# A fused FFN, GRU and expert kernel on one core: the loop over tiles and the loop over weight pieces written out

## The chip, the cores and the metric

The kernel runs on one core of a Trainium2 chip. The metric is the device time of one execution in microseconds (us). Five engines of the core work side by side and meet at semaphores only: TensorE (PE, with its weight loads as PEld), VectorE (DVE), ScalarE (ACT), GpSimd (POOL) and SyncE (SP, which here only issues DMAs).

## What is computed

The reference joins two blocks over x of 16 sequences, 256 steps, 512 features. Cut to what matters:

```python
# block 0: attention over 8 block sums gives one row per sequence; layer norm; FFN on quantised values
proj = attended @ Wo.T
q = layernorm(x + proj) * ln_gamma + ln_beta
inter = silu(q8(q) @ q4(w_gate).T) * (q8(q) @ q4(w_up).T)      # 512 -> 2048
x = x + q8(inter) @ q4(w_down).T                               # 2048 -> 512
# block 1: a GRU over the 256 steps, h is [16, 512]; then a linear layer with routed low-rank experts
for t in range(256):
    gi, gh = x[:, t] @ W_ih + b_ih, h @ W_hh + b_hh
    r, z = sigmoid(gi_r + gh_r), sigmoid(gi_z + gh_z)
    n = tanh(gi_n + r * gh_n)
    h = (1 - z) * n + z * h
    hs[:, t] = h
logits = silu(hs @ rw1.T + rb1) @ rw2.T + rb2 + gates
coeff = softmax of the two largest logits, the rest 0          # 16 experts, rank 16
x = x + hs @ W.T + bias + expand(hs @ A.T, coeff) @ B
```

The 256 steps of the GRU depend on each other one by one; all else can run beside them.

## The kernel before, in words

A tile is 8 time steps times 16 sequences, 128 rows, and there are 32 tiles. The work is a software pipeline over a counter c: while the GRU takes the 8 steps (slots s = 0 to 7) of tile c, the same slots carry quantisation of tile c+4 (flag Q), the FFN of tile c+3 and the end of the FFN of tile c+2 (F, E), the input products `gi` of tile c+1 (I), and the routed experts and output of tile c-1 (L). Flag R says that the GRU itself runs. For c from 1 to 27 all six flags are set.

Each engine has its own program, written in order by one `slot(c, s)` per engine; the order is fixed by hand. In a slot of PE `state_products` comes first: 64 matmuls into `ps_rn` and 32 into `ps_z` (L1299), which need the state parts `hx` of the step before. Behind it stand the other products of the slot. DVE does `beside(0)` (FFN work), then `recur` (r_half L739, r_pre L745, z_pre L755, rn L760, n_pre L762, zn L772, hx L774, and last the low part `hx` L725, which releases the next step on PE and POOL), with `beside(1)` and `beside(2)` inside it, and `beside(3)` at its end. ACT does the tanh of r, z and n, and evictions. POOL copies `hx` into `hT_steps` (L1016), collects a tile in `hT_tile` (L1023, once a tile), multiplies scales into quantised tiles (`qf` L1003, `qx` L1051), and does small steps of the routing (`share` L1035, `c` L1040, `coeff` L1044). SP loads and stores the tiles.

`over_tiles` calls `slot` for c = -3 to 1 as written-out code, then puts one loop on every engine (`engine.Fori(2, TILES - 5)`, so c = 2 to 26, 25 turns, its line in the trace is L275) whose counter is a register, and then c = 27 to 32 written out again. Before that, `over_pieces` quantises and turns the FFN weights in 24 pieces; pieces 8 to 11 stand in a loop of two turns (L293), the others are written out. In a loop every wait is for a value worked out from the counter: `count(c, per_tile, more)`. Where a wait of such a value stands before some instructions, `wait_apart` adds one increment of a semaphore `passed`, which nobody waits for, between the wait and the instruction. These increments are in the written-out tiles too. On DVE they stand before `to_f8` (L799), before `clip` (L806), before `bn_aggr`, `max` and `max_index`; on POOL before both copies of h, before `ve`, `share` and each `c`; on PE before `turn_hid`; on SP before each load and store.

Of the kernel before, what the change touches and what calls it, by code (L numbers as in the profile page):

```python
# [63 lines left out]
def count(tile, per_tile, more=0):  # L64

    if isinstance(tile, int):
        if tile < 0:
            return 0
        if tile >= TILES:
            return TILES * per_tile  # L70
    return tile * per_tile + more


def wait(engine, sem, value):

    if not (isinstance(value, int) and value <= 0):
        engine.wait_ge(sem, value)


def wait_apart(engine, passed):  # L80


    engine.sem_inc(passed, 1)
# [11 lines left out]
def build(nc, x_steps, h0, ident, pick, block_mask, iota, rms_w, query, WkT, WoT, gamma, beta,  # L95
          ffn_w, W_ih, W_hh, b_ih, b_hh, WL, bias, rb1, rw2T, rb2, gates, BT, x1_dram, out):
    with ExitStack() as ctx:
# [164 lines left out]
        passed = sem("passed")  # L262
# [23 lines left out]
        def over_pieces(engine, piece, sums, attention, slot, ahead=0):  # L286
# [35 lines left out]
        def stages(c):  # L322


            if not isinstance(c, int):
                return True, True, True, True, True, True
            return tuple(0 <= c + d < TILES for d in (4, 3, 2, 1, 0, -1))
# [3 lines left out]
        def _(sp):  # L331

            def piece(turn, u):
                wait(sp, w_y, count_piece(turn, u, -1))
                wait_apart(sp, passed)
                at = (turn * 2 + u) * P
                src = ffn_w[at:at + P, :] if isinstance(turn, int) else ffn_w[bass.ds(at, P), :]
                sp.dma_start(wst[u][:, :], src).then_inc(w_loaded[u], 16)

            def loads(c):  # L340
                Q, F, E, I, R, L = stages(c)
                if L:
                    wait(sp, x1b_done, count(c - 1, 1))
                    wait_apart(sp, passed)
                    sp.wait_ge(x1_stored, count(c, 1) * 16)
                    wait_apart(sp, passed)
                    sp.dma_start(x1_in[:, :], rows(x1_dram, c - 1)).then_inc(x1in_loaded, 16)
                if E:
                    wait(sp, x1_done, count(c + 2, 1))
                    wait_apart(sp, passed)  # L350
                    sp.dma_start(xres[:, :], rows(x_steps, c + 2)).then_inc(xres_loaded, 16)

            def load_x_in(q):
                wait(sp, xs_done, count(q, 1))
                wait_apart(sp, passed)
                sp.dma_start(xin[:, :], rows(x_steps, q)).then_inc(xin_loaded, 16)

            def stores(c):
                Q, F, E, I, R, L = stages(c)
                if E:  # L360
                    sp.wait_ge(x1_done, count(c + 2, 1, 1))
                    wait_apart(sp, passed)
                    sp.dma_start(rows(x1_dram, c + 2), x1[:, :]).then_inc(x1_stored, 16)
                if L:
                    sp.wait_ge(y_ok, count(c - 1, 1, 1))
                    wait_apart(sp, passed)
                    sp.dma_start(rows(out, c - 1), y[:, :]).then_inc(y_stored, 16)

            def rows(dram, t):
                if isinstance(t, int):  # L370
                    return dram[t * P:(t + 1) * P, :]
                return dram[bass.ds(t * P, P), :]

            def slot(c, s):
                if s == 0:
                    loads(c)
                    if isinstance(c, int) and c == -4:
                        load_x_in(0)
                if s == 4 and (not isinstance(c, int) or c + 5 < TILES):
                    load_x_in(c + 5)  # L380
                if isinstance(c, int) and c == -4:
# [5 lines left out]
                if isinstance(c, int) and c == -3 and s == STEPS - 2:  # L387
# [8 lines left out]
            over_pieces(sp, piece, nothing, nothing, slot)  # L396
            over_tiles(sp, slot)
# [5 lines left out]
        def _(act):  # L403
# [27 lines left out]
            def piece(turn, u):  # L431
                ps = (ps_up, ps_z)[u]
                act.wait_ge(w_mm, count_piece(turn, u, 1))
                nc.scalar.activation(wq[:, bass.ds(turn * 2 + u, 1), :], ps[:, :].bitcast(BF16).unsqueeze(1),
# [46 lines left out]
            def others(c, s, Q, F, E, I, L):  # L481
# [45 lines left out]
                if I and s in (1, 3, 5):  # L527
                    g = s // 2
                    act.wait_ge(gi_mm, count(i, 3, g + 1))
                    if isinstance(c, int) and c == -1:  # L530
# [6 lines left out]
            def slot(c, s):  # L537
# [9 lines left out]
                if isinstance(c, int) and c in (-3, -2, 0):  # L547
# [3 lines left out]
            over_pieces(act, piece, load_x, attention, slot, ahead=1)  # L551
            over_tiles(act, slot)
# [3 lines left out]
        def _(dve):  # L556
# [16 lines left out]
            def piece(turn, u):  # L573


                if not (isinstance(turn, int) and turn == TURNS - 1 and u == 1):
# [225 lines left out]
            def clip(out, in8, ready, at, used, done):  # L802
                wait(dve, used, at)
                dve.wait_ge(ready, at + 1)
                wait_apart(dve, passed)
# [26 lines left out]
            def others(c, s, place, Q, F, E, I, L):  # L832
# [15 lines left out]
                if L and here == (4, 2):  # L848
                    dve.wait_ge(l_small, count(l, 6, 2))
                    wait_apart(dve, passed)  # L850
                    v.max(top[:, :], lg[:, :]).then_inc(l_small, 1)
                if L and here == (5, 1):
                    dve.wait_ge(l_small, count(l, 6, 3))
                    wait_apart(dve, passed)
# [42 lines left out]
                if Q and here == (1, 0):  # L897
# [5 lines left out]
                    wait_apart(dve, passed)  # L903
# [26 lines left out]
            def slot(c, s):  # L930
# [11 lines left out]
                if isinstance(c, int):  # L942
                    if c == -3:
                        gru_weights(s)
                    if c in (-2, 0):
                        input_weights(c, s)
# [5 lines left out]
            over_pieces(dve, piece, nothing, attention, slot)  # L952
            over_tiles(dve, slot)
# [3 lines left out]
        def _(pool):  # L957
# [22 lines left out]
            def piece(turn, u):  # L980

                if not (isinstance(turn, int) and turn == TURNS - 1 and u == 1):
# [5 lines left out]
            def slot(c, s):  # L988
                Q, F, E, I, R, L = stages(c)
                q, f, e, l = c + 4, c + 3, c + 2, c - 1  # L990
                if Q and s == 0:
                    pool.wait_ge(xin_loaded, count(q, 16, 16))
                    wait(pool, xn_done, count(q, 1))
                    if isinstance(c, int) and c == -4:
# [16 lines left out]
                if R:  # L1011
# [3 lines left out]
                    wait_apart(pool, passed)  # L1015
                    g.tensor_copy(hT_steps[:, :, s, :], hx[:, :, :, :].rearrange("p k u b -> p (k u) b"))\  # L1016
                        .then_inc(hcopy, 1)
                if R and s == STEPS - 1:
# [3 lines left out]
                    wait_apart(pool, passed)  # L1022
# [8 lines left out]
                if L and s == 5:  # L1031
                    pool.wait_ge(gap_ok, count(l, 1, 1))
                    wait_apart(pool, passed)
# [3 lines left out]
                    for place, c_one in enumerate((c0, c1)):  # L1037
                        pool.wait_ge(share_ok, count(l, 2, 2))
                        wait_apart(pool, passed)
# [15 lines left out]
            over_pieces(pool, piece, nothing, attention, slot)  # L1055
            over_tiles(pool, slot)
# [3 lines left out]
        def _(pe):  # L1060
# [156 lines left out]
            def turn_hid(l):  # L1217
                pe.wait_ge(hid_ok, count(l, 1, 1))
                pe.wait_ge(xa_ok, count(l, 1, 1))
                wait_apart(pe, passed)  # L1220
# [101 lines left out]
            def slot(c, s):  # L1322
# [6 lines left out]
                if isinstance(c, int):  # L1329
                    if c in (-3, -2):  # L1330
                        weights_scales(c, s)
                    if (c, s) == (-1, 0):
# [66 lines left out]
```

## Time and profile before

| | |
|---|---|
| time, median of 3 runs | 1940.21 us (1937.06 to 1950.23) |
| time of the profiled execution | 1945.7 us |
| span of the profiled execution, first to last instruction | 1943.9 us |
| PE busy | 1646.0 us, 85% |
| DVE busy | 1597.8 us, 82% |
| ACT and POOL busy | 664.4 us and 654.8 us, 34% each |

The profile divides the span into 40 slices of 48.6 us and gives busy tenths of each engine for a slice. The first six or so are the weights and the attention; from there the tiles run, one in about a slice. A busy PE is not a PE at its peak, since ends of its matmuls are modelled.

### The profile page before, as it was taken

Reading aid. Unit: us, or ns where it says so; the run is one execution under the profiler, and the core shown is the slowest. Engines: PE = TensorE matmul, PEld = TensorE weight load, DVE = VectorE, ACT = ScalarE, POOL = GpSimd, SP = SyncE. Lnnn points to the kernel's source line nnn. Section 1 sums busy time; section 2 is a strip of 40 time slices with the busy share of each in tenths; the row PEclk is TensorE's granted clock in tenths of the full one; section 3 lists DMA queues with packets and bytes.
Section 4 is the critical chain, followed back from the end, with each engine's and each line's share of the span. In section 5 each row is a group of like instructions: output and inputs, shape, how many; then the busy total and the mean of one; then the engine's idle time right before and its main releaser. Section 6 shows DMA issues by size and latency. Waiting matters only on the chain. (4 is left out here: it accounts for less than half of the span.)

```text
span 1943.9 us, 81883 instructions
## 1 busy us (share of the span) xinstructions
PE 1646.0 (85%) x32972; PEld 1247.0 (64%) x32972; DVE 1597.8 (82%) x5651; ACT 664.4 (34%) x1712; POOL 654.8 (34%) x859
## 2 busy tenths in 40 slices
PE   5422348999999999999999999999999999999976
PEld 2211116777777777777777777777777777778864
DVE  8999987888888888888788888888888888887653
ACT  1111224433333333333333333333333333333331
POOL 4555323333333333333323333333333333332111
PEclk8755569999999999999999999999999999999997
DMA  7413120000000000001000000000000000001000
GB/s 254 147 60 125 51 87 24 25 30 31 30 30 30 30 30 27 12 30 30 30 30 30 30 30 25 30 30 30 30 30 30 30 30 17 22 26 32 27 14 18
DMA packets 35405, 80.45 MB, mean 41 GB/s; under 512 B 4864, under 2 KB 5248, under 8 KB 34688
## 3 DMA queue, kind: packets, MB, share of 16 engines
q1 hardware_dynamic: 28080, 63.09, 9.6%
q10 hardware_dynamic: 6992, 12.13, 1.7%
q8 instruction: 306, 5.01, 1.1%
q14 instruction: 27, 0.22, 0.0%
HBM read 58.43 MB, written 16.78 MB: 39 GB/s over the span
## 5 line engine op out<-in xcount | busy, mean ns | idle before, releaser
L1299 PE MATMUL ps_rn<-hx,whh 128*128 128x32 f16 x16384 | 451.1, 176 | 77.1 <-DVE hx L725 47.5
L1299 PEld LDWEIGHTS ps_rn<-hx,whh 128*128 128x128 f16 x16384 | 430.8, 96 | 124.9 <-DVE hx L725 93.7
L1016 POOL COPY hT_steps<-hx 128x128 f16<-128x128 f16 x256 | 120.0, 469 | 978.7 <-DVE hx L725 978.7
L1192 PE MATMUL ps_gi<-x1T,wih 128*128 128x128 f16 x4608 | 288.6, 219 | 1.2 <-ACT gi L533 1.2
L1192 PEld LDWEIGHTS ps_gi<-x1T,wih 128*128 128x128 f16 x4608 | 270.3, 98 | 25.7 <-issue 1.7
L542 ACT ACTIVATE r_tanh<-r_pre,scale_half 128x64 f32<-128x64 f32 x256 | 89.0, 348 | 563.3 <-DVE r_pre L745 563.3
L1299 PE MATMUL ps_z<-hx,whh 128*128 128x32 f16 x8192 | 244.0, 176 | 0.0
L1299 PEld LDWEIGHTS ps_z<-hx,whh 128*128 128x128 f16 x8192 | 223.4, 96 | 0.0
L533 ACT ACTIVATE gi<-ps_gi,b_i,scale_x 128x128 f32 (+1 forms) x384 | 144.7, 457 | 166.2 <-PE ps_gi L1192 166.2
L1003 POOL TENSOR_TENSOR qf<-f8c,fe 128x512 bf16<-128x512 bf16 x128 | 135.8, 1061 | 119.3 <-DVE f8c L806 102.7
L1125 PE MATMUL ps_gate_up<-wq,qxT 128*128 128x512 bf16 x512 | 144.2, 398 | 32.3 <-issue 19.8
L739 DVE TENSOR_TENSOR r_half<-ps_rn,gi 128x64 f32<-128x64 f32 x256 | 55.9, 218 | 111.5 <-PE ps_rn L1299 111.0
L1131 PE MATMUL ps_gate_up<-wq,qxT 128*128 128x512 bf16 x512 | 136.3, 390 | 1.7 <-ACT sg_gs L493 1.7
L1149 PE MATMUL ps_down<-wq,qfT 128*128 128x512 bf16 x512 | 134.8, 386 | 0.0
L544 ACT ACTIVATE z_tanh<-z_pre,scale_half 128x64 f32<-128x64 f32 x256 | 89.0, 348 | 123.7 <-DVE z_pre L755 123.7
L806 DVE TENSOR_SCALAR f8c<-f 128x512 bf16<-128x512 fp8e4 x128 | 109.8, 858 | 17.8 <-DVE f L799 0.2
L546 ACT ACTIVATE n<-n_pre,scale_half 128x64 f32<-128x64 f32 x256 | 89.1, 348 | 57.5 <-DVE n_pre L762 44.0
L762 DVE SCALAR_TENSOR_TENSOR n_pre<-gi,rn 128x64 f32<-128x64 f32 x256 | 75.7, 296 | 30.6 <-DVE rn L760 0.2
L1201 PE MATMUL ps_base<-wl,hT_tile 128*128 128x512 f16 x384 | 98.0, 393 | 0.0
L799 DVE SCALAR_TENSOR_TENSOR f<-inter,finv 128x512 fp8e4<-128x512 f32 x128 | 94.0, 734 | 0.3
L821 DVE TENSOR_TENSOR inter<-ps_gate_up,sg_gs 128x512 f32<-128x512 f32 x128 | 87.8, 686 | 7.2 <-PE ps_gate_up L1131 7.1
L493 ACT ACTIVATE sg_gs<-ps_gate_up 128x512 f32<-128x512 f32 x128 | 74.7, 583 | 53.4 <-PE ps_gate_up L1125 53.3
(197 smaller groups left out, 2765.5 us busy)
## 6 DMA issues: line engine op xcount, KB each, us to landing
wih<-in_x_steps ACTq DMA_DIRECT2D x32, 256.0 KB, 5.4
xin<-in_x_steps SPq DMA_DIRECT2D x32, 256.0 KB, 4.1
xres<-in_x_steps SPq DMA_DIRECT2D x32, 256.0 KB, 4.1
x_dram<-x SPq DMA_DIRECT2D x32, 256.0 KB, 2.8
x_in<-x_dram SPq DMA_DIRECT2D x32, 256.0 KB, 2.8
out_rows<-y SPq DMA_DIRECT2D x32, 256.0 KB, 2.0
wst<-in_ffn_w SPq DMA_DIRECT2D x12, 512.0 KB, 3.2
sg_gs<-in_ffn_w SPq DMA_DIRECT2D x12, 512.0 KB, 3.5
```

The lines of the kernel that those rows point to most:

```text
L533: last = nc.scalar.activation(gi_gate(i, g)[:, k, :], ps_gi[:, k * P:(k + 1) * P], ACT.Identity, bias=b_i[:, g * KD + k:g * KD + k + 1], s ...
L546: nc.scalar.activation(n[:, :], n_pre[:, :], ACT.Tanh, scale=HALF_S_INV).then_inc(n_ok, 1)
L799: v.scalar_tensor_tensor(blocked(out8[:, :]), blocked(src[:, :]), TO_F8, spread(inverse[:, :]), ALU.mult, ALU.mult, saturate=False).then_i ...
L806: v.tensor_scalar(out[:, :], in8[:, :], 7.5 / 64, -7.5 / 64, ALU.min, ALU.max).then_inc(done, 1)
L1003: g.tensor_tensor(blocked(qf[:, :]), blocked(f8c[:, :]), spread(fe16[:, :]), ALU.mult).then_inc(qf_done, 1)
L1016: g.tensor_copy(hT_steps[:, :, s, :], hx[:, :, :, :].rearrange("p k u b -> p (k u) b"))\
L1125: last = mm(ps_gate[:, :], qxT[:, k, :], w_ffn(0, n, k), start=k == 0, stop=k == KD - 1)
L1131: last = mm(ps_up[:, :], qxT[:, k, :], w_ffn(8, n, k), start=k == 0, stop=k == KD - 1)
L1149: last = mm(ps_down[:, :], qfT[:, i, :], w_down(i), start=i == 0, stop=i == NF * KD - 1)
L1192: last = mm(ps_gi[:, j * P:(j + 1) * P], wih_parts[:, k, at:at + P], x1T[:, x, k, :], start=k + w + x == 0, stop=k == KD - 1 and w == 1)
L1201: last = mm(out, hT_tile[:, 2 * k + x, :], wl_parts[:, k, begin:begin + n], start=k + w + x == 0, stop=stop and w == 1)
L1299: last = mm(ps[:, (at + j) * 2 * B:(at + j + 1) * 2 * B], whh[:, k, u, gate * D + j * P:gate * D + (j + 1) * P], hx[:, k, :, :].rearrange( ...
```

## The change

The loops on the engines become Python loops, so all 25 turns of the tile loop and both turns of the piece loop are written out as code. No counter register is left: every wait is for a constant. `wait_apart` and the semaphore `passed` are gone, everywhere. No instruction that computes is added, removed or moved. The core of the diff; the same lines go at the other places named above:

```diff
 def wait(engine, sem, value):
 
-    if not (isinstance(value, int) and value <= 0):
+    if value > 0:
         engine.wait_ge(sem, value)
-
-
-def wait_apart(engine, passed):
-
-
-    engine.sem_inc(passed, 1)
...
-        def over_tiles(engine, slot):
-
-            def all_slots(c):
+        def over_tiles(slot):
+
+            for c in range(-3, TILES + 1):
                 for s in range(STEPS):
                     slot(c, s)
 
-            for c in range(-3, 2):
-                all_slots(c)
-            with engine.Fori(2, TILES - 5) as c:
-                all_slots(c)
-            for c in range(TILES - 5, TILES + 1):
-                all_slots(c)
...
-            with engine.Fori(SUM_PARTS // 2, TURNS // 2) as turn:
-                piece(turn, 0)
-                piece(turn, 1)
+            for p in range(SUM_PARTS, PIECES // 2):
+                piece(p // 2, p % 2)
...
-            if isinstance(c, int):
-                at = (c % 2 * 3 + gate) * D
-                part = gi[:, at:at + D]
-            else:
-                part = gi[:, bass.ds((c & 1) * (3 * D) + gate * D, D)]
+            at = (c % 2 * 3 + gate) * D
+            part = gi[:, at:at + D]
...
                 if E:
                     wait(sp, x1_done, count(c + 2, 1))
-                    wait_apart(sp, passed)
                     sp.dma_start(xres[:, :], rows(x_steps, c + 2)).then_inc(xres_loaded, 16)
...
             def clip(out, in8, ready, at, used, done):
                 wait(dve, used, at)
                 dve.wait_ge(ready, at + 1)
-                wait_apart(dve, passed)
                 v.tensor_scalar(out[:, :], in8[:, :], 7.5 / 64, -7.5 / 64, ALU.min, ALU.max).then_inc(done, 1)
...
                     for place, c_one in enumerate((c0, c1)):
                         pool.wait_ge(share_ok, count(l, 2, 2))
-                        wait_apart(pool, passed)
                         g.tensor_scalar(c_one[:, :], iota_b[:, :], at_f[:, place:place + 1], share[:, place:place + 1],
```

PE, end of a turn and start of the next slot: `x_row` gives the spread scale, `bt` the experts, `x` and `qx` are turned, and `ps_rn` opens the next step. Before, at the end of the loop's body (what follows the branch here is the code behind the loop; a taken branch goes back to such a `ps_rn` row at the top):

```order
L1129 REGISTER_ALU
L1131 MATMUL ps_gate_up<-wq,qxT 128x512 x4
L1169 MATMUL ps_turn<-idf,x 128x128 x4
L1149 MATMUL ps_down<-wq,qfT 128x512 x4
L1173 REGISTER_ALU
L1180 MATMUL ps_route<-idb,qx 128x128 x4
L275 REGISTER_ALU
L275 COMPARE_AND_BRANCH
L1299 MATMUL ps_rn<-hx,whh 128x32 x64
```

The same place in the changed kernel, which now stands there once for each tile:

```order
L1089 MATMUL ps_gate_up<-wq,qxT 128x512 x4
L1127 MATMUL ps_turn<-idf,x 128x128 x4
L1107 MATMUL ps_down<-wq,qfT 128x512 x4
L1138 MATMUL ps_route<-idb,qx 128x128 x4
L1256 MATMUL ps_rn<-hx,whh 128x32 x64
```

The matmuls are the same in the same order; register work and branch are gone. PE's body has 27 rows of register work, a loop's frame included.

DVE, the recurrence of one step inside the loop before:

```order
L739 ISA
L739 TENSOR_TENSOR r_half<-ps_rn,gi 128x64
L741 TENSOR_TENSOR hn_half<-ps_rn,b_h 128x64
L745 TENSOR_TENSOR r_pre<-ps_rn,r_half 128x64
L748 TENSOR_TENSOR hn<-ps_rn,hn_half 128x64
L752 ISA
L752 TENSOR_TENSOR z_half<-ps_z,gi 128x64
L755 TENSOR_TENSOR z_pre<-ps_z,z_half 128x64
L760 SCALAR_TENSOR_TENSOR rn<-r_tanh,hn 128x64
L762 ISA
L762 SCALAR_TENSOR_TENSOR n_pre<-gi,rn 128x64
```

And the same rows of the changed kernel:

```order
L708 TENSOR_TENSOR r_half<-ps_rn,gi 128x64
L710 TENSOR_TENSOR hn_half<-ps_rn,b_h 128x64
L714 TENSOR_TENSOR r_pre<-ps_rn,r_half 128x64
L717 TENSOR_TENSOR hn<-ps_rn,hn_half 128x64
L721 TENSOR_TENSOR z_half<-ps_z,gi 128x64
L724 TENSOR_TENSOR z_pre<-ps_z,z_half 128x64
L729 SCALAR_TENSOR_TENSOR rn<-r_tanh,hn 128x64
L731 SCALAR_TENSOR_TENSOR n_pre<-gi,rn 128x64
```

An ISA row here is register work on the counter. In the body of DVE's loop 70 of 239 rows are register work or the branch; the other 169 stand in the changed kernel once for each tile. Increments of `passed` have no rows in this listing.

## Rows read from the trace of the kernel before

**Rows 1.** The page: busy tenths of PE in 40 slices, and TensorE's granted clock.
```profile
PE   5422348999999999999999999999999999999976
...
PEclk8755569999999999999999999999999999999997
```
**Rows 2.** Who waited for whom: engine, line, releaser, us in total, times, longest.
```profile
PEld ps_rn L1299 <- DVE hx L725: 93.7, 131, 2.5
```
**Rows 3.** DVE in order of time, L725 only: start, us, engine, line, operation.
```profile
369.27 0.22 DVE L725 TENSOR_TENSOR hx<-h,hx 128x64 f16<-128x64 f32 x1
...
398.18 0.22 DVE L725 TENSOR_TENSOR hx<-h,hx 128x64 f16<-128x64 f32 x1
...
403.55 0.23 DVE L725 TENSOR_TENSOR hx<-h,hx 128x64 f16<-128x64 f32 x1
...
415.59 0.22 DVE L725 TENSOR_TENSOR hx<-h,hx 128x64 f16<-128x64 f32 x1
...
464.78 0.22 DVE L725 TENSOR_TENSOR hx<-h,hx 128x64 f16<-128x64 f32 x1
...
1699.24 0.23 DVE L725 TENSOR_TENSOR hx<-h,hx 128x64 f16<-128x64 f32 x1
...
1729.71 0.22 DVE L725 TENSOR_TENSOR hx<-h,hx 128x64 f16<-128x64 f32 x1
...
1735.43 0.22 DVE L725 TENSOR_TENSOR hx<-h,hx 128x64 f16<-128x64 f32 x1
...
1747.46 0.22 DVE L725 TENSOR_TENSOR hx<-h,hx 128x64 f16<-128x64 f32 x1
```
**Rows 4.** Stretch of tile 27: us, busy us of PE, PEld, DVE, ACT, POOL, clock, DMA.
```profile
1699.50:1747.70 48.20, 47.13 (x1021) 37.35 (x1020) 41.85 (x169) 19.20 (x52) 16.98 (x25) 1.00 0.08 25
```
**Rows 5.** The loops' lines: durations ns min/median/max, first and last start us.
```profile
L275 PEldq COMPARE_BRANCH  x25: 76/3430/3915, 464.3 to 1698.8; - x25
...
L275 DVEq COMPARE_BRANCH  x25: 50/56/74, 466.7 to 1701.2; - x25
...
L293 PEldq COMPARE_BRANCH  x2: 76/162/247, 91.4 to 108.2; - x2
```
**Rows 6.** PE in order of time behind the loop's branch, a turn's end.
```profile
1085.42 0.39 PE L1180 MATMUL ps_route<-idb,qx 128*128 128x128 bf16 x4
1086.72 1.76 PE L1299 MATMUL ps_rn<-hx,whh 128*128 128x32 f16 x64 [0.91 <-issue]
```
**Rows 7.** PE in order of time at the same place in written-out code.
```profile
1749.52 0.39 PE L1180 MATMUL ps_route<-idb,qx 128*128 128x128 bf16 x4
1749.74 1.75 PE L1299 MATMUL ps_rn<-hx,whh 128*128 128x32 f16 x64
```
**Rows 8.** DVE in order of time, tile 27, with its waits.
```profile
1718.06 0.68 DVE L799 SCALAR_TENSOR_TENSOR f<-inter,finv 128x512 fp8e4<-128x512 f32 x1
1718.88 1.53 DVE L806 TENSOR_SCALAR f8c<-f 128x512 bf16<-128x512 fp8e4 x1
...
1724.35 0.68 DVE L821 TENSOR_TENSOR inter<-ps_gate_up,sg_gs 128x512 f32<-128x512 f32 x1
1725.07 0.69 DVE L780 TENSOR_REDUCE fam<-inter 128x16 f32<-128x512 f32 x1
...
1733.17 0.09 DVE L855 MATCH_VALUE_LOAD top_at<-top,lg 128x8 f32 x1 [0.26 <-issue]
...
1737.89 1.47 DVE L863 TENSOR_TENSOR wxa<-xa,coeff 128x256 f32<-128x256 f32 x1 [0.56 <-POOL coeff L1044]
```
**Rows 9.** The page, DMA queues that bring instructions: packets, MB, share.
```profile
q8 instruction: 306, 5.01, 1.1%
q14 instruction: 27, 0.22, 0.0%
```
**Rows 10.** POOL in order of time, tile 27.
```profile
1718.86 1.27 POOL L1028 TENSOR_TENSOR xg<-xn,gamma_b 128x512 f32<-128x512 f32 x1
...
1721.50 1.05 POOL L1003 TENSOR_TENSOR qf<-f8c,fe 128x512 bf16<-128x512 bf16 x1
...
1736.69 0.86 POOL L1040 TENSOR_SCALAR c<-iota_b,at_f,share 128x16 f32<-128x16 f32 x2 [0.21 <-POOL share L1035]
```
**Rows 11.** Line L806: durations ns min/median/max, first and last start.
```profile
L806 DVE TENSOR_SCALAR f8c<-f x128: 426/428/1542, 232.0 to 1802.6; 128x512 bf16<-128x512 fp8e4 x128
```

More of the change, by code:

```diff
@@ L284, in count_piece, with over_pieces @@
             return turn * 2 + (u + more)
-        def over_pieces(engine, piece, sums, attention, slot, ahead=0):
+        def over_pieces(piece, sums, attention, slot, ahead=0):
             for p in range(SUM_PARTS):
@@ L376, in slot @@
                     loads(c)
-                    if isinstance(c, int) and c == -4:
+                    if c == -4:
                         load_x_in(0)
-                if s == 4 and (not isinstance(c, int) or c + 5 < TILES):
+                if s == 4 and c + 5 < TILES:
                     load_x_in(c + 5)
-                if isinstance(c, int) and c == -4:
+                if c == -4:
                     if s == 3:
@@ L394, in slot @@
                     stores(c)
-            over_pieces(sp, piece, nothing, nothing, slot)
-            over_tiles(sp, slot)
+            over_pieces(piece, nothing, nothing, slot)
+            over_tiles(slot)
             sp.wait_ge(y_stored, 16 * TILES)
@@ L546, in slot @@
                     nc.scalar.activation(n[:, :], n_pre[:, :], ACT.Tanh, scale=HALF_S_INV).then_inc(n_ok, 1)
-                if isinstance(c, int) and c in (-3, -2, 0):
+                if c in (-3, -2, 0):
                     weights(c, s)
                 others(c, s, Q, F, E, I, L)
-            over_pieces(act, piece, load_x, attention, slot, ahead=1)
-            over_tiles(act, slot)
+            over_pieces(piece, load_x, attention, slot, ahead=1)
+            over_tiles(slot)
         @block.vector
@@ L573, in piece @@
             def piece(turn, u):
-                if not (isinstance(turn, int) and turn == TURNS - 1 and u == 1):
+                if not (turn == TURNS - 1 and u == 1):
                     scales(turn + u, 1 - u)
@@ L951, in _ @@
             scales(0, 0)
-            over_pieces(dve, piece, nothing, attention, slot)
-            over_tiles(dve, slot)
+            over_pieces(piece, nothing, attention, slot)
+            over_tiles(slot)
         @block.gpsimd
@@ L980, in piece @@
             def piece(turn, u):
-                if not (isinstance(turn, int) and turn == TURNS - 1 and u == 1):
+                if not (turn == TURNS - 1 and u == 1):
                     scale_piece(turn + u, 1 - u)
@@ L1054, in _ @@
             scale_piece(0, 0)
-            over_pieces(pool, piece, nothing, attention, slot)
-            over_tiles(pool, slot)
+            over_pieces(piece, nothing, attention, slot)
+            over_tiles(slot)
         @block.tensor
@@ L1328, in slot @@
                     state_products(ps_z, 0, GATE_Z).then_inc(z_mm, 1)
[L1329 to L1332, printed above, removed]
-                        pe.wait_ge(wih_lo, KD)
-                    if (c, s) == (1, 0):
-                        pe.wait_ge(wl_lo, KD)
-                        pe.wait_ge(bt_loaded, 16)
+                if c in (-3, -2):
+                    weights_scales(c, s)
+                if (c, s) == (-1, 0):
+                    pe.wait_ge(wih_lo, KD)
+                if (c, s) == (1, 0):
+                    pe.wait_ge(wl_lo, KD)
+                    pe.wait_ge(bt_loaded, 16)
                 others(c, s, Q, F, E, I, L)
             pe.wait_ge(c_dve, 1)
-            over_pieces(pe, piece, block_sums, attention, slot, ahead=1)
+            over_pieces(piece, block_sums, attention, slot, ahead=1)
             pe.wait_ge(w_ev, PIECES)
-            over_tiles(pe, slot)
+            over_tiles(slot)
 def kernel(x, cond_2048, L0_cond_rms_weight, L0_cond_Wk, L0_cond_Wo, L0_cond_ln_gamma, L0_cond_ln_beta,
```

51 lines of the change are left out of this document (14 added, 37 removed).

## The prediction, made before the changed kernel was run

> **What bounds the kernel now.** I read the slices first. From the seventh on PE is busy nine tenths or more at full clock, where DVE shows eight [rows 1]; the table of waits then tells who closes the circle: PE waits for `hx` of DVE 131 times, but only for 93.7 us in all [rows 2]. So the tiles are a circle between PE and DVE in which now the one, now the other is late, and any time that both lose goes straight into the span. What matters is then the length of a tile. The low part `hx` (L725) ends each GRU step, so eight of its rows make a tile, and I took its starts from DVE's rows in order of time [rows 3]:
>
> - tile 1, written out, 369.27 to 415.59: 46.32 us;
> - tile 2, first turn of the loop, 415.59 to 464.78: 49.19 us;
> - tiles 3 to 26, the 24 turns behind a taken branch, 464.78 to 1699.24: 1234.46 us, 51.44 each;
> - tile 27, written out again, 1699.24 to 1747.46: 48.22 us.
>
> All these tiles carry the same matmuls and vector work, but tile 1 follows a tile without the output part, and its first step is short for that. So tile 27 is the fair price of a written-out tile: 3.2 us less than a turn of the loop. It is also near its floor: in it PE is busy for 47.13 of 48.20 us, at full clock [rows 4].
>
> **The change part by part.** *The branch.* On PE a taken branch has a median of 3430 ns, while the last, untaken one takes 76; on DVE the branch takes 56 ns whether or not it is taken [rows 5]. Behind it PE stands idle for 0.91 us before `ps_rn`, waiting for nothing the profile shows, after the work queued ahead of the branch has run out [rows 6]; at the same place in written-out code `ps_rn` starts with no idle time, on the heels of the products before it [rows 7]. On the path, the branch costs what tiles 3 to 26 have over tile 2: 51.44 - 49.19 = 2.25 us. The part of the 3.4 us that costs nothing is covered by the matmuls in the queue. 24 x 2.25 = 54 us go.
>
> The Trainium skill, Advanced Engine Details and Errata, section Control Flow Timing, puts a compare-and-branch at about 108 ns. By that, 24 branches would be worth 2.6 us instead of 54, and this change little. The trace bears it out on DVE and not on PE.
>
> *Register work.* 70 of 239 rows of DVE's body and 27 of PE's go. Most of it is hidden behind the instruction that runs; the path pays what tile 2 has over tile 27: 49.19 - 48.22 = 0.97 us, 25 x 0.97 = 24 us. Both together are 1234.46 + 49.19 - 25 x 48.22 = 78 us.
>
> *More code.* What comes in its place is code that each engine must be sent. In tile 27 DVE idles 0.26 us before L855 for no wait that the profile names [rows 8]; that step, 1729.71 to 1735.43, takes 5.72 us, and the same step of tile 1, 398.18 to 403.55, takes 5.37 [rows 3]. I take these 0.35 us for a new block of instructions. So 48.22 already holds one such stall. With none a tile would be 47.87, with two 48.57: 25 tiles make this 9 us either way. PE's queue brought 306 blocks and the one of the others only 27 [rows 9]; the latter number must rise about threefold, since DVE's and ACT's loops were fetched once and are now fetched 25 times. I keep one exposed stall a tile, because most will fall where the engine has work queued or waits anyway.
>
> The Trainium skill, Runtime: NRT & Kernel Launch, section Instruction fetch mechanics, says that crossing a block is "mostly hidden". By it the sum would be the lower of these, 9 us less.
>
> *Increments of `passed`.* These cost in tile 27 too, and go in all tiles. On DVE `f8c` (L806) follows `f` (L799), which it needs, 0.14 us after its end; `fam` (L780) follows `inter` (L821), which it needs just so and without an increment, after 0.04 us [rows 8]. One increment on a fresh result costs 0.10 us. On POOL the first `c` starts 0.21 us after `share` [rows 10], with two increments between. Where do they lie on the path? Slots 0, 1 and 2 end with PE: nothing gained. In slot 3 and 7 `f8c` is held by POOL's work, not by the increment (below): nothing. In slot 5 I count one for `clip` and one for `max_index`: 0.2 us. In slot 6 DVE waits 0.56 us for `coeff` before `wxa` [rows 8], and the copy, `share` and both `c` of POOL before it have increments: the 0.21 us fall to about 0.1, and the copy starts 0.1 earlier: 0.2 us. That is 0.4 us a tile. It needs slots that DVE ends, and PE has 48.20 - 47.13 = 1.07 us of idle time to give [rows 4], so there is room. Over some 31 tiles it is 12 us; bounds are nothing and all of PE's 1.07, 0 to 33 us.
>
> *The piece loop and SP.* PE's taken branch there costs 247 ns at most [rows 5], behind DVE's work: 0. SP's increments stand ahead of DMAs issued tens of us early: 0.
>
> Sum: 1943.9 - 78 - 12 = 1854 us of span, 1856 with the 1.8 us around it. The profiled run, 1945.7 us, is 5.5 above the median of the three timed, and the turns of the loop are the part whose length varies, so a part of these 5.5 us goes with them and a part does not. I take 1853.
>
> **The rivals.**
>
> *The order at the port of DVE and POOL turns.* `f8c` takes 428 ns in the median but up to 1542 [rows 11]. In slot 3 it starts at 1718.88 and ends at 1720.41, and POOL's `xg` multiply runs from 1718.86 to 1720.13 [rows 8, 10]: the long ones wait for a POOL operation that began 20 ns earlier. The 0.10 us of the increment are enough to turn this. If `f8c` goes first it ends about 1.1 us earlier, but PE's `ps_rn` still needs 1.75 us [rows 7], so DVE gains 0.3 us at most in slots 3 and 7: 31 x 0.6 = 19 us, to 1834. Or the two `xg` and `qf` of POOL move back by the 0.43 us of `f8c`, and `n_pre`, which must be done before `hx`, is held by them: a loss of about 0.35 us in a slot, 31 x 0.7 = 22 us, to 1875. The Trainium skill, GPSIMD Engine Reference, section Specifications, names the shared interface and that DVE instructions of two SBUF inputs or a 2-port mode contend there; it does not say who wins. I give each turn one chance in ten.
>
> *The increments cost nothing on the path*, since PE takes over as the bound at once: 1853 + 12 = 1865. One in eight.
>
> *The loop is not what makes its tiles long*, or the new code's fetches cost as much: 1940. Against it: the untaken branch costs 76 ns, the tiles behind it are short at once, and tiles 1 and 27 lie 1300 us apart and agree step by step. 3 in 100.
>
> *Slower.* The place is DVE's, ACT's and POOL's own fetching. A loop tile has 3.2 us over a written-out one, and each exposed stall costs 0.35 us, so it would take 9 more of them in a tile than tile 27 shows, or one stall as long as PE's branch, 3.4 us, per tile. Then 25 x 3.9 us lead to about 1955. Tile 27 is 48.22 with code that arrives in just this way, so 2 in 100.
>
> **How the numbers follow.** The forecast has 0.62 (own range 1843 to 1862, from 9 us either way of the stalls), the turns 0.1 each (1834 and 1875), the idle increments 0.13, no gain 0.03, slower 0.02. The range 1834 to 1874 leaves about 0.15 outside. Measured on this kernel, 1% (19 us) is about what can be told from no change; all cases but the last two lie over 3% below: faster 0.95, same 0.03, slower 0.02.
>
> **What would show it.** No branch rows; `ps_rn` behind the turned `qx` with no idle time; tiles of 47.6 to 48.2 us by `hx` from tile 2 to 27, all nearly alike; `f8c` 0.04 us behind `f`; the gap before the first `c` about 0.1; some 60 packets more in the queue that had 27, and fewer in PE's. It would be wrong if tiles in the middle were longer than 49 us, if idle time for "issue" on DVE or ACT came several times in a tile, or if slots 3 and 7 changed by more than 0.3 us.

## The result, and the profile after

The changed kernel takes 1867.03 us (median of four runs, 1865.47 to 1868.51), the kernel before beside it 1939.33 us. The ratio is 0.9616, with a 95% interval from 0.9579 to 0.9654: faster by 72 us, where 86 were forecast (1853 us). The profiled execution took 1865.47 us, its span is 1863.5 us, 80.4 less than before. The page of the changed kernel: the span, the busy time of each engine, TensorE's granted clock in 40 slices, and the two queues that bring instructions:

```profile
span 1863.5 us, 77042 instructions
...
PE 1620.1 (87%) x32972; PEld 1246.9 (67%) x32972; DVE 1540.8 (83%) x5651; ACT 661.9 (36%) x1712; POOL 676.2 (36%) x859
...
PEclk8755569999999999999999999999999999999996
...
q8 instruction: 259, 4.24, 0.9%
q14 instruction: 83, 0.68, 0.1%
```

The work is the same, 32972 matmuls and 5651 DVE operations. PE's queue brought 47 blocks less than in [rows 9] and the other queue 56 more.

The low part of h, in order of time on DVE, answers to [rows 3]; line 694 is L725 before. The first two rows bound tile 2, the last two tile 27:

```profile
413.93 0.22 DVE L694 TENSOR_TENSOR hx<-h,hx 128x64 f16<-128x64 f32 x1
...
462.13 0.23 DVE L694 TENSOR_TENSOR hx<-h,hx 128x64 f16<-128x64 f32 x1
...
1619.83 0.22 DVE L694 TENSOR_TENSOR hx<-h,hx 128x64 f16<-128x64 f32 x1
...
1668.03 0.22 DVE L694 TENSOR_TENSOR hx<-h,hx 128x64 f16<-128x64 f32 x1
```

Both tiles take 48.20 us. Tiles 2 to 26 go from 413.93 to 1619.83, 1205.90 us or 48.24 each; before they took 1699.24 - 415.59 = 1283.65. That is 77.8 of the 80.4 us; the head up to tile 2 gives 1.7 (415.59 to 413.93), tile 27 nothing, the rest behind it about 1.

On PE, at the place of [rows 6] where a turn's end stood:

```profile
1090.84 0.39 PE L1138 MATMUL ps_route<-idb,qx 128*128 128x128 bf16 x4
1091.06 1.75 PE L1256 MATMUL ps_rn<-hx,whh 128*128 128x32 f16 x64
```

`ps_rn` now follows the turned `qx` at once, as in [rows 7].

Slots differ, though, from tile 27 of before. From such rows, slots 0 to 7 of a tile in the middle take 7.16, 5.62, 6.23, 6.50, 5.52, 5.34, 6.90 and 4.93 us; 17 of the 26 tiles agree with that within 0.02 us a tile. Slot 3 has got longer than in tile 27 before (6.30), and it is the slot in which DVE and POOL meet. DVE and then POOL in that slot, tile 20, beginning at 1301.1 us:

```profile
1301.01 0.68 DVE L767 SCALAR_TENSOR_TENSOR f<-inter,finv 128x512 fp8e4<-128x512 f32 x1
1301.80 0.43 DVE L773 TENSOR_SCALAR f8c<-f 128x512 bf16<-128x512 fp8e4 x1
...
1304.15 0.64 DVE L729 SCALAR_TENSOR_TENSOR rn<-r_tanh,hn 128x64 f32<-128x64 f32 x1
1304.83 0.97 DVE L731 SCALAR_TENSOR_TENSOR n_pre<-gi,rn 128x64 f32<-128x64 f32 x1
```
```profile
1301.15 0.70 POOL L977 COPY hT_steps<-hx 128x128 f16<-128x128 f16 x1 [5.93 <-DVE hx L694]
1301.81 1.55 POOL L988 TENSOR_TENSOR xg<-xn,gamma_b 128x512 f32<-128x512 f32 x1
1303.44 1.27 POOL L990 TENSOR_TENSOR xg<-xg,beta_b 128x512 f32<-128x512 f32 x1
1304.67 1.05 POOL L966 TENSOR_TENSOR qf<-f8c,fe 128x512 bf16<-128x512 bf16 x1
```

The same two DVE operations in tile 27 before, in the slot of [rows 8, 10]:

```profile
1721.30 0.33 DVE L760 SCALAR_TENSOR_TENSOR rn<-r_tanh,hn 128x64 f32<-128x64 f32 x1
1721.66 0.97 DVE L762 SCALAR_TENSOR_TENSOR n_pre<-gi,rn 128x64 f32<-128x64 f32 x1
```

Where [rows 8, 10] had `xg` 20 ns ahead, `f8c` is now 10 ns ahead and takes 0.43 us instead of 1.53, and `xg` takes 1.55 instead of 1.27. But POOL's add and `qf` come later for it. `rn` (0.64, before 0.33) ends just after the add, and `n_pre` just after `qf`, at 1305.80 against 1305.72. `n_pre` took 0.97 us before too, but it now ends 4.79 us behind the start of `f`, where it ended 4.57 behind it. The turn at the port that the prediction named as a rival has happened: the 1.1 us won by `f8c` are lost again, and 0.2 us more.

### The profile page after: what moved, and what is told of

Same layout as the page of the kernel before. It is cut to its first block, busy times and chain, and to the rows that moved or that the text cites. A ratio compares the mean times of both kernels' runs of the same rounds, so it can differ in the third digit from the quotient of the medians.

```text
span 1863.5 us, 77042 instructions
## 1 busy us (share of the span) xinstructions
PE 1620.1 (87%) x32972; PEld 1246.9 (67%) x32972; DVE 1540.8 (83%) x5651; ACT 661.9 (36%) x1712; POOL 676.2 (36%) x859
## 4 chain that ended last, share of the span: by engine, by line
PE 47%; DVE 41%; issue 7%; POOL 3%; DMA 1%; ACT 1%; DVEq 0%; POOLq 0%; ACTq 0%; SPq 0%
PE ps_rn L1256 15%; PE ps_gi L1150 7%; PE ps_z L1256 7%; PE ps_gate_up L1089 3%; PE ps_base L1203 3%; PE ps_down L1107 3%; PE ps_gate_up L1083 3%; PE ps_route L1159 3%; DVE wxa L828 2%; DVE rn L729 2%; DVE less_z L737 2%; DVE zn L741 2%; DVE hx L743 2%; DVE gi L557 2%; DVE gi L554 1%
## 5 line engine op out<-in xcount | busy, mean ns | idle before, releaser
L977 POOL COPY hT_steps<-hx 128x128 f16<-128x128 f16 x256 | 127.6, 498 | 928.2 <-DVE hx L694 928.2
L502 ACT ACTIVATE gi<-ps_gi,b_i,scale_x 128x128 f32<-128x128 f32 x384 | 144.7, 457 | 164.4 <-PE ps_gi L1150 164.4
L1083 PE MATMUL ps_gate_up<-wq,qxT 128*128 128x512 bf16 x512 | 137.0, 391 | 14.1 <-DVE inter L788 14.1
L1089 PE MATMUL ps_gate_up<-wq,qxT 128*128 128x512 bf16 x512 | 136.7, 391 | 2.1 <-ACT sg_gs L462 2.1
L749 DVE TENSOR_REDUCE fam<-inter 128x16 f32<-128x512 f32 x128 | 87.9, 687 | 4.4
```

Source lines behind the costliest of these rows:

```text
L502: last = nc.scalar.activation(gi_gate(i, g)[:, k, :], ps_gi[:, k * P:(k + 1) * P], ACT.Identity, bias=b_i[:, g * KD + k:g * KD + k + 1], s ...
L1083: last = mm(ps_gate[:, :], qxT[:, k, :], w_ffn(0, n, k), start=k == 0, stop=k == KD - 1)
L1089: last = mm(ps_up[:, :], qxT[:, k, :], w_ffn(8, n, k), start=k == 0, stop=k == KD - 1)
```

## The experiments

They were timed in three sets on two chips, each set beside the kernel before, which took 1946.93, 1944.22 and 1942.44 us there. Times of different sets differ by a few us for that reason, so the sizes of steps are read from the traces, where most slots repeat within 0.02 us from tile to tile.

**Only the loops go.** Both loops written out, the increments kept.

```diff
-            for c in range(-3, 2):
-                all_slots(c)
-            with engine.Fori(2, TILES - 5) as c:
-                all_slots(c)
-            for c in range(TILES - 5, TILES + 1):
+            for c in range(-3, TILES + 1):
                 all_slots(c)
...
-            with engine.Fori(SUM_PARTS // 2, TURNS // 2) as turn:
-                piece(turn, 0)
-                piece(turn, 1)
+            for p in range(SUM_PARTS, PIECES // 2):
+                piece(p // 2, p % 2)
```

> Both loops written out, the increments of `passed` kept: only the loops go. Theory 1 (from the changed kernel's steps): the loops alone are worth all of the gain, 78 us, and the increments nothing, because slots 7, 0, 1 and 2 end with PE and slot 3 got longer when they went. Tiles 2 to 27 then are 48.0 to 48.2 us, slot 3 6.30 us (6.50 without the increments), slot 6 7.01 (6.90), and the time 1862 to 1868 us, within 0.3% of the changed kernel. Theory 2 (the forecast): the increments cost 0.4 us a tile, so this kernel is slower than the changed one by 8 to 12 us, 1875 to 1879 us.

Measured: 1868.9 us beside 1946.93, ratio 0.9594 (0.9547 to 0.964): 78 us less, the whole gain and the forecast's term for the loops. A tile takes 48.11 us in most turns, slots 7.07, 5.64, 6.21, 6.30, 5.51, 5.37, 7.01, 5.01. So the increments, all together, give nothing in the tiles: a tile is 0.09 us longer without them. Theory 1 holds there. Of the profiled spans, 1866.2 and 1863.5 us, the changed kernel's is still the shorter, by 3.7 us ahead of tile 2 and behind tile 27. That isn't put down to the increments: the start of tile 2 lies anywhere from 411.9 to 419.4 us in the kernels of this text. Its `f8c`, DVE in order of time in slot 3:

```profile
1302.24 0.68 DVE L794 SCALAR_TENSOR_TENSOR f<-inter,finv 128x512 fp8e4<-128x512 f32 x1
1303.06 1.54 DVE L801 TENSOR_SCALAR f8c<-f 128x512 bf16<-128x512 fp8e4 x1
```

It starts 0.14 us behind `f`, in the changed kernel 0.11 us. The increment itself was worth 0.03 us there, not 0.10: `f8c` waits for two semaphores, and in both kernels the trace has a semaphore instruction on DVE between `f` and it, which `fam` does not have.

**Fewer turns.** The loop kept, with more tiles in a turn: five tiles and 5 turns, or twelve tiles and 2 turns.

```diff
-            with engine.Fori(2, TILES - 5) as c:
-                all_slots(c)
+            with engine.Fori(0, 5) as turn:
+                for k in range(5):
+                    all_slots(turn * 5 + (k + 2))
```

> The tile loop kept with registers and increments, but five tiles in a turn: 5 turns instead of 25. Theory 1 (a taken branch on PE costs 2.25 us, register work 0.97 us a tile): 21 taken branches fewer (4 instead of 24, and one tile less behind one) save 45 us, so 1895 us; 4 times the steps of slot 0 and 1 are long, 21 tiles are 49.2 us. Rival (register work is most of it, a branch is cheap): 1930 us. Second rival: a body of five tiles no longer stays with DVE, ACT and POOL between turns, so their branches take microseconds too instead of 56 ns, and a turn's start costs more than 2.25 us, but as there are only 4 that is under 10 us.

> Twelve tiles in a turn, 2 turns (tiles 2 to 25), the rest written out, registers and increments kept: one taken branch. Theory 1: 24 tiles pay 0.97 us of register work and one pays a branch, so 24 + 2 us over the written-out kernel: 1890 to 1893 us; the difference to five tiles in a turn, 3 branches and one tile of register work, is 8 us. Rival (register work is most of the loop's price): 1925 us or more.

Measured: five tiles a turn 1901.47 us, ratio 0.9751 (0.9702 to 0.98); twelve 1878.31 us, 0.9641 (0.9594 to 0.9687). The line of the loop in both, durations of the branch in ns as in [rows 5], first with five tiles a turn, then with twelve:

```profile
L275 PEldq COMPARE_BRANCH  x5: 83/3825/3933, 661.1 to 1655.6; - x5
...
L275 DVEq COMPARE_BRANCH  x5: 55/63/74, 663.5 to 1658.0; - x5
```
```profile
L275 PEldq COMPARE_BRANCH  x2: 83/1789/3495, 996.0 to 1579.7; - x2
...
L275 DVEq COMPARE_BRANCH  x2: 55/59/63, 998.5 to 1582.3; - x2
```

A taken branch keeps its price on PE when it is rare, 3.3 to 3.9 us. DVE's own branch row stays short, but the time behind it does not. `x1T`, the last operation of a turn, and `inter`, the first of the next, on DVE: first in the kernel before, then with five tiles a turn, then with twelve, and last POOL's first operation behind its branch with twelve:

```profile
1085.48 0.75 DVE L927 SCALAR_TENSOR_TENSOR x1T<-ps_turn,scale_x,x1T 128x512 f16<-128x512 f32 x1 [0.93 <-ACT x1T L520]
1086.15 0.68 DVE L821 TENSOR_TENSOR inter<-ps_gate_up,sg_gs 128x512 f32<-128x512 f32 x1
...
1162.16 0.75 DVE L928 SCALAR_TENSOR_TENSOR x1T<-ps_turn,scale_x,x1T 128x512 f16<-128x512 f32 x1 [0.97 <-ACT x1T L521]
1165.41 0.69 DVE L822 TENSOR_TENSOR inter<-ps_gate_up,sg_gs 128x512 f32<-128x512 f32 x1 [2.49 <-issue]
...
998.46 0.75 DVE L928 SCALAR_TENSOR_TENSOR x1T<-ps_turn,scale_x,x1T 128x512 f16<-128x512 f32 x1 [1.15 <-ACT x1T L521]
1001.64 0.69 DVE L822 TENSOR_TENSOR inter<-ps_gate_up,sg_gs 128x512 f32<-128x512 f32 x1 [2.42 <-issue]
...
1000.45 1.27 POOL L997 TENSOR_TENSOR xs<-xin,proj 128x512 f32<-128x512 f32 x1 [2.10 <-issue]
```

With one tile a turn DVE goes on at once; with five or twelve it stands idle for 2.4 to 2.5 us and waits for nothing that the profile shows. So the second rival came true: a longer body makes the branches of the other engines cost microseconds too. With five tiles a turn, tiles that follow no branch take 48.95 to 49.25 us, 0.95 more than written out: the register work, as forecast. The four behind a branch make up 13.5 us in all, 3.4 each and not 2.25, and the kernel is 6 us over the 1895 of theory 1. Two things lie in that: the stall of DVE, and TensorE's clock. Two of the four tiles (53.91 and 52.09 us) have a stretch of 3.4 us in which TensorE was granted 1.2 instead of 2.4 GHz; the other two take 52.22 and 51.10. How much is due to each is not separated.

With twelve tiles a turn the one tile behind a branch takes 50.45 us, 2.15 more than its neighbours. The register work itself is smaller: most tiles take 48.3 to 48.8 us, 0.4 more than written out, and the trace has 914 register instructions on DVE instead of 1788. Over 24 tiles that accounts for the 12 us by which this kernel comes out under its expectation. How the register work is shared out in a body of twelve tiles was not looked into.

**Each engine's part.** The tile loop written out on PE alone (below, where `out` writes out tiles -3 to 32), and on all engines but PE.

```diff
-        def over_tiles(engine, slot):
+        def over_tiles(engine, slot, out=False):
...
+            if out:
+                for c in range(-3, TILES + 1):
+                    all_slots(c)
+                return
...
-            over_tiles(pe, slot)
+            over_tiles(pe, slot, out=True)
```

> The kernel before with PE's tile loop alone written out; DVE, ACT, POOL and SP keep their loop of 25 turns with registers, and the increments stay. Theory 1 (the branch costs on PE alone, the register work on the others): PE's 54 us go and the register work of DVE stays, 0.97 us a tile, so 24 us over the fully written-out kernel with increments (1869): 1890 to 1896 us. Rival (the branch of any engine makes the pause): 1935 us or more.

> The reverse: PE keeps its loop, all other engines have the tiles written out, increments stay. Theory 1: the 24 taken branches of PE cost 2.25 us each on the path and perhaps a little more, since the others no longer pay for their registers: 1869 + 54 = 1923 us, 1915 to 1930. Its steps of slot 0 and 1 stay 8 and 6.5 to 7 us long, those of slots 2 to 7 are as in the written-out kernel. Rival (the register work of the others is most of it): 1895 us or less.

Measured: PE alone written out 1888.04 us, ratio 0.9722 (0.9704 to 0.9739); PE alone in a loop 1926.04 us, 0.9914 (0.9897 to 0.9931). PE's branch in the second, and DVE's in the first:

```profile
L279 PEldq COMPARE_BRANCH  x25: 76/3643/3797, 463.4 to 1678.6; - x25
```
```profile
L279 DVEq COMPARE_BRANCH  x25: 50/56/74, 468.0 to 1643.2; - x25
```

With PE written out, 2 us under the expectation, a tile takes 48.97 us, in 24 of 25 turns alike: the branches of four engines and all their register work are 0.86 us a tile over 48.11. With PE alone in the loop, slots 2 to 7 are those of the written-out kernel and slots 0 and 1 take 8.1 and 6.9 us: 24 tiles of 50.63 us, 2.5 over the 48.15 of the first turn. With one tile a turn the pause is PE's alone. This is the cleanest split of the 78 us. Read from the starts of tiles 2 to 27, PE's loop is worth 59 us either way (its 27 rows of register work go with the branch and aren't separated from it), and the loops of the others 20 to 22 us (0.86 us a tile, or the kernel before against PE alone in the loop). By the device times it is 54 to 57 and 16 to 19.

**The piece loop.** As the first experiment, with the loop over weight pieces kept.

> Increments kept, tile loop written out, the loop of two turns over weight pieces 8 to 11 kept with its registers. Both theories: the piece loop stands behind DVE's work, 8.2 us a piece, so it is worth under 1 us: 1866 to 1871 us, the same as with everything written out and the increments kept (1869). Rival: PE's branch of 247 ns and four register rows a piece show up as 1 to 3 us.

Measured: 1870.52 us, ratio 0.9616 (0.96 to 0.9632). The kernel with everything written out and the increments kept had 1868.9 us in another set, ratio 0.9594 (0.9547 to 0.964). Within what can be told apart the piece loop costs nothing.

**One increment back.** The changed kernel with the increment before `clip` alone.

```diff
             def clip(out, in8, ready, at, used, done):
                 wait(dve, used, at)
                 dve.wait_ge(ready, at + 1)
+                dve.sem_inc(passed, 1)
```

> The changed kernel with one kind of increment back, that before `clip` (L806 before) on DVE, five a tile. Theory 1 (order at the port): `f8c` starts late enough again for POOL's `xg` multiply and `qx` to go first; `f8c` is about 1.5 us long in slot 3 and 1.3 us in slot 7 instead of 0.43, slot 3 is 6.3 us instead of 6.50, slot 7 5.0 instead of 4.93; the time falls by 0 to 5 us, or stays. Rival (slot 3 is long for another reason, as POOL's earlier copy): slot 3 stays at 6.50 and the time is the same or 1 us longer.

Measured: 1862.09 us, ratio 0.9553 (0.9505 to 0.96). That is not told apart from the changed kernel's 0.9616 (0.9579 to 0.9654) by the times, but by the traces: a tile takes 48.01 us against 48.20, slots 3 and 7 are 6.29 and 5.01, and `f8c` is long again. DVE in slot 3:

```profile
1300.78 0.68 DVE L768 SCALAR_TENSOR_TENSOR f<-inter,finv 128x512 fp8e4<-128x512 f32 x1
1301.59 1.54 DVE L775 TENSOR_SCALAR f8c<-f 128x512 bf16<-128x512 fp8e4 x1
...
1304.01 0.33 DVE L730 SCALAR_TENSOR_TENSOR rn<-r_tanh,hn 128x64 f32<-128x64 f32 x1
1304.37 0.97 DVE L732 SCALAR_TENSOR_TENSOR n_pre<-gi,rn 128x64 f32<-128x64 f32 x1
```

An instruction that does nothing, put back, takes 0.19 us off a tile, because it gives POOL the first turn. That settles what lengthened slot 3.

**POOL's work out of DVE's way.** Three orders on POOL, on top of the changed kernel. First both `xg` operations ahead of the copy of `hx` that ends slot 2:

```diff
+                if Q and s == 2:
+                    pool.wait_ge(xn_done, count(q, 1, 1))
+                    wait(pool, q8_done, count(q, 1))
+                    g.tensor_tensor(xg[:, :], xn[:, :], gamma_b[:, :], ALU.mult).then_inc(xg_done, 1)
+                    pool.wait_ge(xg_done, count(q, 1, 1))
+                    g.tensor_tensor(xg[:, :], xg[:, :], beta_b[:, :], ALU.add).then_inc(xb_done, 1)
                 if R:
                     pool.wait_ge(hx_ok, c * STEPS + (s + 2))
...
-                if Q and s == 2:
...
```

> The changed kernel with one order changed on POOL: the two `xg` operations of slot 2 (L988 and L990, 1.3 us each alone) stand ahead of the copy of `hx` that ends the slot instead of behind it, so they run in slot 2, and `qf` follows the copy at once. Theory 1 (slot 3 is long because DVE's `rn` and `n_pre`, which read SBUF twice, are held by POOL's `xg` and `qf`): in slot 3 `n_pre` falls from 970 to 230 ns, `rn` from 640 to 230, slot 3 from 6.50 to 5.0 to 5.3 us; PE's own work then makes slot 4 longer, so a tile falls by 0.6 to 0.9 us, 28 tiles, 1842 to 1850 us. Rival (slot 3 is PE's or DVE's own length): no change, 1867. Second rival: the `xg` operations now hold DVE in slot 2, whose length rises from 6.23 by as much as slot 3 loses.

Measured: 1868.62 us, ratio 0.9615 (0.9599 to 0.963): no gain. Slot 3 fell to 5.33 us as expected, slot 4 rose to 6.02, and slot 2 rose to 6.98, which is the second rival. DVE and POOL in slot 2:

```profile
1300.31 0.92 DVE L756 TENSOR_SCALAR fe<-fam 128x16 f32<-128x16 f32 x1
```
```profile
1299.92 1.27 POOL L978 TENSOR_TENSOR xg<-xg,beta_b 128x512 f32<-128x512 f32 x1
```

`fe`, 16 elements and 0.17 us elsewhere, ends at 1301.23, just behind the add at 1301.19.

Then `x_bias` moved from slot 5, behind `coeff`, to slot 4:

```diff
+                if L and s == 4:
+                    pool.wait_ge(x1in_loaded, count(l, 16, 16))
+                    wait(pool, y_ok, count(l, 1))
+                    g.tensor_tensor(x1_bias[:, :], x1_in[:, :], bias_b[:, :], ALU.add).then_inc(x1b_done, 1)
                 if R:
                     pool.wait_ge(hx_ok, c * STEPS + (s + 2))
```

> The changed kernel with POOL's `x_bias` (L1005, 1.27 us) moved from the end of slot 5, where it stands behind `coeff`, to slot 4, ahead of its copy, where POOL is idle for 4 us. Theory 1 (`wxa` on DVE is 1.48 us because it reads SBUF twice and is held until `x_bias` ends): `wxa` falls to 0.3 to 0.5 us, slot 6 from 6.90 to 6.0 or less, and a tile by 0.5 to 1.0 us, where PE becomes the bound (it has about 1 us of idle time a tile): 1838 to 1853 us. Rival (`wxa` is that long by itself, 256 elements): no change.

Measured: 1842.63 us, ratio 0.9481 (0.9465 to 0.9497). `wxa` on DVE, first in the changed kernel, then here:

```profile
1320.57 1.48 DVE L828 TENSOR_TENSOR wxa<-xa,coeff 128x256 f32<-128x256 f32 x1 [0.45 <-POOL coeff L1002]
```
```profile
1305.84 0.43 DVE L828 TENSOR_TENSOR wxa<-xa,coeff 128x256 f32<-128x256 f32 x1 [0.44 <-POOL coeff L1006]
```

1.05 us of `wxa` was waiting for `x_bias`. Slot 6 falls from 6.90 to 5.82 and slot 7 rises from 4.93 to 5.29, a tile is 47.47 us. The changed kernel shows the same without any edit in tile 4, where `x_bias` happens to start 0.10 us behind `wxa` and not ahead of it; slot 6 is 6.21 us there and the tile 47.51:

```profile
549.04 0.43 DVE L828 TENSOR_TENSOR wxa<-xa,coeff 128x256 f32<-128x256 f32 x1 [0.45 <-POOL coeff L1002]
```
```profile
549.14 1.46 POOL L1005 TENSOR_TENSOR x_bias<-x_in,bias_b 128x512 f32<-128x512 f32 x1
```

Both moves together:

> Both moves on POOL together. Theory 1: their gains don't add up fully, since PE is busy for 47.1 us of a tile: tiles of 47.2 to 47.5 us instead of 48.20, so about 28 us off, 1835 to 1845 us, with hardly any idle time of PE before `ps_rn`. Rival (gains add up): under 1830 us.

Measured: 1845.58 us, ratio 0.9491 (0.9478 to 0.9504), tiles of 47.59 us, at the upper end of what was expected. The first move still gives nothing.

So only the multiply of `xg` was put ahead of the copy, with `x_bias` in slot 4:

> `x_bias` in slot 4, as in the run before, and of the two `xg` operations only the multiply ahead of the copy that ends slot 2; the add stays behind it. With both ahead, slot 2 grew from 6.23 to 6.98, because DVE's `fe` (0.92 us instead of 0.17) was held until the add ended; the multiply alone ends at 3.14 us in the slot, before `fe` at 3.6. Theory 1: slot 2 stays 6.23, the add ends at 2.3 us in slot 3 and `qf` at 3.3, so slot 3 is 5.3 to 5.6 instead of 6.50 and slot 4 5.8 to 6.0 instead of 5.51; a tile 46.7 to 47.0 instead of 47.47, so 1823 to 1832 us. Rival (PE's work, 47.1 us a tile, is the floor and gives nothing more): 1840 us.

Measured: 1825.01 us, ratio 0.9399 (0.9384 to 0.9415). Slot 2 stays 6.22, slots 3 and 4 are 5.41 and 5.95, a tile is 46.83 us. A stretch of one tile, first in the changed kernel, then here, in the columns of [rows 4]:

```profile
1282.10:1330.30 48.20, 47.31 (x1023) 37.45 (x1022) 40.44 (x169) 19.20 (x52) 17.95 (x25) 1.00 0.09 31
```
```profile
1300.00:1346.80 46.80, 46.80 (x1027) 37.59 (x1023) 38.19 (x168) 19.20 (x52) 17.92 (x26) 1.00 0.09 31
```

PE shows no idle time in a tile any more, though ends of its matmuls are modelled. This is the fastest version here, 2.3% below the changed kernel.

Last, `x_bias` in slot 4 and the increment before `clip`:

> `x_bias` in slot 4 and the increment before `clip` put back. If the two gains add up: slot 3 6.30 and slot 6 5.83, a tile 47.3 instead of 47.47, the time 1836 to 1841 us, 2 to 5 us under `x_bias` alone. Rival (slots 3 to 6 have become PE's): the same as `x_bias` alone, 1843.

Measured: 1834.47 us, ratio 0.9444 (0.9429 to 0.946), tiles of 47.28 us. The gain of a tile, 0.19 us, adds to that of `x_bias`; the time is 2 us under the expectation.

## Why the prediction was right or wrong

The 1867 us lie 14 above the forecast of 1853 and 5 above the range that belonged to it (1843 to 1862); they are inside the wider range only because that allowed for the rivals. What the loops cost was right; what the increments cost was not.

*The frame was right.* Tile 27 was the fair price of a tile: 48.22 us forecast, 48.20 measured (in part by luck, see below), and 78 us for the loops, 77.8 measured in the traces and 78 in the kernel that has only the loops written out.

*The branch*, 54 us: right. Written out on PE alone, with registers elsewhere, the tiles lose 2.4 us, and PE alone in a loop keeps 2.5 a branch. The forecast left out that a part of this is TensorE's clock. In the kernel before, four of the 24 tiles behind a taken branch have a stretch of 3.4 us at 1.2 GHz, 5 to 8 us behind the tile's start; here is one, in the columns of [rows 4]:

```profile
777.80:781.20 3.40, 2.81 (x29) 1.34 (x26) 3.01 (x18) 1.39 (x4) 0.05 (x1) 0.50 0.06 21
```

These four tiles cost 3.2 us over tile 2, the other 20 cost 2.05. Between 400 and 1750 us such stretches stand in three traces, all of kernels with PE in a loop (the one before, five tiles a turn, PE alone in the loop), and in none where PE's tiles are written out.

The 108 ns of the Trainium skill, Advanced Engine Details and Errata, section Control Flow Timing, are twice what DVE's row shows (56 ns) and far off PE's (3.3 to 3.9 us). The Trainium skill, Runtime: NRT & Kernel Launch, section Instruction fetch mechanics, gives a reason: a taken branch to code outside the fetched window fetches its target first. The traces agree in two points. PE's queue brought 259 blocks in every kernel with PE's tiles written out, 306 with 24 taken branches, 267 with four and 263 with one. And whether an engine waits goes with how long its body is, counted in the trace from branch to branch:

| engine, tiles a turn | instructions in the body | from the branch's end to the next row |
|---|---|---|
| DVE, 1 / 5 / 12 | 285 / 1393 / 3018 | 0.24 / 2.8 to 3.0 / 2.8 us |
| ACT, 1 / 5 / 12 | 95 / 459 / 940 | 0.21 / 2.5 to 3.2 / 3.9 us |
| POOL, 1 / 5 / 12 | 67 / 327 / 768 | 0.12 / 0.21 to 0.25 / 2.8 us |

The next row is register work, which waits for nothing. PE's body of one tile has 2080 instructions and pays already; there the profile puts the stall into the branch's own row. The blocks fetched at a branch were not followed one by one.

*Register work*, 24 us: nearly right, 20 to 22.

*More code*: the forecast kept one exposed stall of 0.35 us a tile. Of tiles 2 to 27 the changed kernel has seven over 48.25 us, by 0.08 to 0.35 over the usual 48.20, 1.6 us together. The number of blocks was right (56 more, forecast 60), their exposure was not: even if all of the 1.6 us is theirs, it is 0.06 us a tile, not 0.35. Here the "mostly hidden" of the Trainium skill, Runtime: NRT & Kernel Launch, section Instruction fetch mechanics, was nearer. The error was covered: without that stall tile 27 would be 47.87, but in its place came slots 0 and 1. They take 7.16 and 5.62 us (6.93 and 5.52 in tile 27 before, 7.07 and 5.64 with the loops out and the increments kept). A slot 0 is longer where the slot 7 ahead of it is shorter: together they take 12.09 us in the changed kernel, 12.08 with the increments kept, and 12.19 ahead of and in tile 27 before, whose slot 0 followed a turn of the loop with a slot 7 of 5.26 us. That PE, still busy, takes the time back fits this but was not tested by itself. So two errors of some 0.3 us a tile, in opposite directions, made 48.2; that was luck.

*The increments*, 12 us: this is the step that failed. "One increment on a fresh result costs 0.10 us" was read from two gaps, 0.14 and 0.04 us, which differ in more than the increment: `f8c` waits for two semaphores and `fam` for one. Without the increment the gap of `f8c` is still 0.11 us, so 0.07 of it is not the increment's. (On POOL the gap before the first `c` did fall from 0.21 to 0.10 us, as forecast.) Slot 5 gave 0.03 us instead of 0.2. Slot 6 gave 0.11 instead of 0.2: the first `c` moved up as forecast, but POOL's copy, starting earlier, now met `q8c` of DVE and took 0.42 us instead of 0.34. Slot 7 gave 0.08, which slot 0 takes back. Slot 3 cost 0.20. The sum is -0.09 us a tile instead of +0.4. That, 25 to 31 tiles of 0.4 to 0.5 us, is the 12 to 14 us between 1853 and 1867.

*The rivals.* "The order at the port turns" came true with a chance of one in ten on either side, and both sides at once: `f8c` goes first, slot 7 gains (0.08, forecast 0.3 at most) and slot 3 loses (0.20, forecast 0.35). "The increments cost nothing on the path" gives 1865, the measured time within 2 us, though by another way than PE taking over alone. The starts 20 ns apart in [rows 8, 10] said that any shift would decide this turn; one in ten for each side was too little for an edit that shifts one of them.

## What to carry to other kernels

Where a loop stands beside the same code written out, the trace has its price already: compare whole periods, and take the written-out one only behind another written-out one. Price an instruction from two gaps only if they differ in it alone, number of waits included. A branch row of some 50 ns does not show that the branch is cheap: look at how long the engine stands idle behind it. Where two engines share a way to memory, look for operations that are longer than their size asks and end just behind another engine's: moving the other engine's work was worth 42 us here, more than half of what the loops were.

## What the runs showed of the hardware

PE's taken branch takes 3.3 to 3.9 us with bodies of one, five or twelve tiles. The branch rows of the others take 40 to 74 ns, but DVE and ACT go on only 2.5 to 3.9 us behind them with five or twelve tiles in the body, and POOL 2.8 us with twelve. DVE operations of two SBUF inputs, and `tensor_scalar` from SBUF, were held by a POOL operation that ran, however small they are: 64 elements took 0.97 us instead of 0.23, 16 elements 0.92 instead of 0.17, 256 elements 1.48 instead of 0.43. Those with an input in PSUM, such as `r_half` at 0.22 us, were not seen to wait. It works the other way too: POOL's multiply took 1.55 us instead of 1.27 when `f8c` came first. The Trainium skill, GPSIMD Engine Reference, section Specifications, names this contention for two SBUF inputs or a 2-port mode. The trace agrees for two SBUF inputs; whether `f8c` and `fe`, with one each, run in such a mode it does not tell. It also shows that the one that came first, by 10 or 20 ns, kept the way until it ended. The granted clock was 2.4 GHz in tiles 2 to 27 of the changed kernel, where the kernel before had four stretches of 3.4 us at 1.2 GHz in its loop.
